# A ViT-tower kernel on one core: mixing rows on GpSimd, weight preparation spread over five prologue tiles, ballast matmuls in tile 0, energy sums ahead of the first projections

## The chip, the core and the metric

The kernel runs on one core of a Trainium2 chip, as one launch. The metric is the device time in microseconds of that core. The engines are TensorE (PE in the profile, its weight loads PEld), VectorE (DVE), ScalarE (ACT), GpSimd (POOL) and the DMA queues, of which SyncE's (SP) and ScalarE's are used. The engines run apart from each other and meet at semaphores only. Each executes its instructions in the order in which they were issued.

## What is computed

The input x has the shape (8, 512, 64, 2): 8 batches of 512 tokens with two feature sets of 64 channels, called ecg and pcg. Three stages follow each other.

```python
# stage 1: four attentions with head size D = 8 over 512 tokens
ecg_out = attn(ecg@w4, pcg@w5, pcg@w6) + alpha * attn(ecg@w1, ecg@w2, ecg@w3)
pcg_out = attn(pcg@w10, ecg@w11, ecg@w12) + gamma * attn(pcg@w7, pcg@w8, pcg@w9)
h = concatenate([ecg_out, pcg_out])                      # (8, 512, 128)
# stage 2: a reservoir and a state-space branch, on x_norm = ln(layernorm(h)), H = 256
new = tanh(xin[t] + prev @ W_res.T); prev = 0.95 * new + 0.05 * prev      # 512 steps in order
A_bar = exp(A * softplus(x_norm @ w_delta + b_delta)); B_bar = (x_norm @ W_B.T) * (1 - A_bar) / (A + 1e-8)
s = A_bar * s + B_bar
readout(s) = gelu(ln(s) @ W_ro.T + b_ro)
h = h + readout(reservoir) * gate + readout(ssm) * (1 - gate)   # gate = sigmoid(layernorm(h) @ W_gate.T + b_gate)
# stage 3: h = h + ffn(layernorm(h)); on 128 channels its additions to the output fall outside,
# and what the kernel adds for it is the normalized h
```

Alpha and gamma are inputs, b_delta too. The whole stage 2 hangs on 512 steps of the reservoir, each of which needs the one before.

## The kernel before, in words

The tokens are cut into 32 tiles of 128 tokens (8 batches times 4 quarters, the quarter outermost, so the first 8 tiles are one of each batch). For each tile the four attentions are computed on all 512 keys. The 512 steps of the reservoir then run in 32 bodies of 16 steps. Step by step TensorE, ScalarE and VectorE pass the state round, and the attention of a tile nine bodies ahead (AHEAD = 9) is laid between the steps. So nine tiles have to be made, all or in part, before the first step: that is the prologue, lines 985 to 1050 for VectorE and 1371 to 1452 for TensorE.

**The opening.** Five transfers bring the weights of the projections (wall), x by batches, the weights of stage 2 (mats) and a row of small inputs (rows, with alpha, gamma, b_delta and the reservoir's A). TensorE begins with 7 matmuls on zeros (`keep_clock`, line 1197, called ballast here: what they write is read by nothing). Then it sums the squares of the wall over the partitions. `project(b, k)` makes for batch b the queries (k = 0), keys (1) and values (2, 3) in one of two banks that alternate; it waits until VectorE has taken what lay in that bank (`stacked`). `sum_energy` adds the squares of x that ScalarE made in `square`. From this energy and the wall's norms come the scales of a batch: VectorE (`squared_scales`), GpSimd (`root`, a power of -1/2) and VectorE again (`scales`). Only then may ScalarE evacuate the batch's projections (`evacuate` waits for `scaled`). This goes for batch 0 alone first, group 1, and then for batches 1 to 7 together, group 2.

**A prologue tile j** (line 1009 for VectorE, 1395 for TensorE, 562 for ScalarE, 415 for GpSimd). `queries(j)` on VectorE subtracts the row shift from the queries, `turn_scores(j)` makes the turned scores with 16 matmuls (line 1221), ScalarE exponentiates each of the four heads twice, once to 32 bits (`prob`, line 516) and once to 16 (`prob_hi`, line 521), GpSimd subtracts them (`low_part`, line 389), and TensorE weighs the values with both parts (`weigh_high`, `weigh_low`). `sums_inverse` and `coefficients` scale the result by the mix of the two attentions: `mix_s[b]` is the row (alpha, 1, gamma, 1) over the scale of batch b, made in `mixes` by VectorE before the loop. Between these, VectorE finds the row maxima of the next tile (`top_of(j + 1, a)`, line 803), normalizes the tile before (`hat`, `hat_copy`, `normed`, `difference`), takes its gate (`gate_in`), and stacks the projections of batches j + 1 and j + 2. TensorE makes those projections in the same tile, with 6 ballast matmuls of 256 columns from tile 1 on.

**The preparation of the weights of stage 2** is on VectorE too. `row_bounds`, `all_bounds` and `take_bounds` find a bound of the weights. In tile 0, behind the third row maximum, come `prepare_weights` (lines 727 to 739: 1 over A, b_t, the readout weights times their gains, the first states of the scan) and `weight_scales` (lines 763 to 779: fifteen instructions on one column each, most of which wait for the one before through `seq`). In tile 1, behind `gate_in`, comes `weight_parts` (line 781: the identity of the carry, W_res in a high and a low half, W_in). `sum_readout` on TensorE and `readout_weights` on VectorE make the readout weights in tile 7. ScalarE and TensorE wait for `wt_ready` to reach 2 before the first step, that is, for the last of weight_parts and of readout_weights.

## Time and profile before

| | |
|---|---|
| median of 3 runs | 684.28 us (681.66 to 684.32) |
| profiled execution | 684.84 us, span 683.1 us |
| mean granted clock of TensorE | 0.959 of full |
| busy: TensorE, VectorE, ScalarE, GpSimd | 627.2, 569.6, 423.9, 192.4 us |
| chain that ended last: TensorE, VectorE, GpSimd, issue, ScalarE | 64, 12, 10, 7, 5 % |
| first fill of the scan (TensorE, line 1303) | 126.07 us |

The page gives the busy time of each engine, the chain of waits that ended last and the costliest groups. The trace behind it is read as a timeline, each line an instruction or a run of the same ones (its start, its busy time, how many, and in brackets how long the engine sat idle before it and what ended the wait), or as windows, stretches with the busy time of each engine and the granted clock of TensorE (1.00 is 2.4 GHz, 0.50 is 1.2 GHz). Neighbouring instructions of an engine overlap by the length of their latency, so the distance of two starts is what an instruction takes from its engine.

### The profile page before, as it was taken

The page shows a single profiled execution, that of the slowest core. Times are in us where ns is not written, and L with a number is a line of the kernel's source. Part 1 is how long each engine was busy: PE and PEld are TensorE (multiplying, and loading weights), DVE is VectorE, ACT ScalarE, POOL GpSimd, SP SyncE. Part 2 cuts the span into 40 slices and gives each one's busy share as a digit, 9 for nine tenths or more (in the row PEclk, how much of TensorE's full clock was granted, in tenths as well). Part 3 has the DMA queues.
Part 4 walks back from the last instruction along what each step waited for, and adds up shares of the span by engine and source line. Part 5 has one row for each costly group of instructions (what it writes and reads, how often), then busy time and mean ns, then how long its engine had stood idle before and what let it go on. Part 6 is the DMA issues. An engine that isn't in the chain of part 4 may idle for free.

```text
span 683.1 us, 28149 instructions
## 1 busy us (share of the span) xinstructions
PE 627.2 (92%) x11038; PEld 489.8 (72%) x11038; DVE 569.6 (83%) x2438; ACT 423.9 (62%) x2051; POOL 192.4 (28%) x429
## 2 busy tenths in 40 slices
PE   7778887999999999999999999999999999999762
PEld 2344554688888888888888888888887777777541
DVE  5778988688888889988998998997667888888895
ACT  4547986577766777766777776676564444444332
POOL 1233655000000000000010000001000778877776
PEclk9659998899999999999999999999999999999997
DMA  5000000000000000000000000000000000000000
GB/s 196 1 0 1 3 1 1 2 3 3 4 3 3 3 3 3 4 3 4 3 4 3 3 4 3 3 3 3 2 2 2 10 14 14 15 17 14 14 21 23
DMA packets 6324, 7.24 MB, mean 11 GB/s; under 512 B 688, under 2 KB 4784, under 8 KB 6192
## 3 DMA queue, kind: packets, MB, share of 16 engines
q1 hardware_dynamic: 5904, 4.46, 2.1%
q8 instruction: 87, 1.43, 0.9%
q10 hardware_dynamic: 288, 0.99, 0.4%
q14 instruction: 45, 0.37, 0.2%
HBM read 3.35 MB, written 2.10 MB: 8 GB/s over the span
## 4 chain that ended last, share of the span: by engine, by line
PE 64%; DVE 12%; POOL 10%; issue 7%; ACT 5%; DMA 1%; POOLq 0%; DVEq 0%; SPq 0%
PE PS L1285 23%; PE PS L1339 13%; PE PS L1297 4%; PE PS L1303 2%; PE PS L1209 2%; PE PS L1234 2%; POOL r_dev L459 2%; PE PS L1235 2%; PE PS L1241 2%; PE PS L1175 2%; PE PS L1179 2%; POOL ln_small L447 2%; PE PS L1292 2%; DVE k L1129 1%; PE PS L1198 1%
## 5 line engine op out<-in xcount | busy, mean ns | idle before, releaser
L548 ACT ACTIVATE y<-PS 128x16 f16<-128x16 f32 x512 | 93.8, 183 | 170.0 <-PE PS L1297 167.1
L1339 PE MATMUL PS<-ballast,ident 128*128 128x220 f16 (+5 forms) x722 | 151.4, 285 | 0.0
L921 DVE TENSOR_TENSOR y_lo<-ys,y 128x16 f16<-128x16 f32 x512 | 95.4, 186 | 52.6 <-ACT ys L549 48.5
L1285 PE MATMUL PS<-y_lo,res_hi 128*128 128x8 f16 x2048 | 128.7, 169 | 9.2 <-DVE y_lo L921 7.3
L1285 PEld LDWEIGHTS PS<-y,res_hi 128*128 128x128 f16 x2048 | 96.9, 97 | 55.6 <-ACT y L548 21.4
L1285 PE MATMUL PS<-y,res_hi 128*128 128x8 f16 x2048 | 129.0, 169 | 0.4 <-ACT y L548 0.3
L1285 PE MATMUL PS<-y,res_lo 128*128 128x8 f16 x2048 | 123.5, 166 | 0.0
L924 DVE SCALAR_TENSOR_TENSOR kp_lo<-PS,setup,kp 128x16 f16<-128x16 f32 x512 | 114.8, 224 | 0.0
L394 POOL TENSOR_TENSOR small<-small,minus_half 128x2 f32<-128x2 f32 x32 | 22.5, 702 | 321.5 <-DVE y_lo L921 284.9
L516 ACT ACTIVATE prob<-PS,exp_up,sc 128x512 f32<-128x512 f32 x128 | 100.3, 790 | 2.1 <-PE PS L1221 2.1
L521 ACT ACTIVATE prob_hi<-PS,exp_up,sc 128x512 f16<-128x512 f32 x128 | 100.5, 792 | 0.0
L549 ACT ACTIVATE ys<-PS 128x16 f32<-128x16 f32 x512 | 99.2, 194 | 0.0
L1285 PEld LDWEIGHTS PS<-y_lo,res_hi 128*128 128x128 f16 x2048 | 85.5, 96 | 18.8 <-DVE y_lo L921 13.8
L551 ACT ACTIVATE kp<-PS 128x16 f16<-128x16 f32 x512 | 98.3, 192 | 0.0
L803 DVE TENSOR_REDUCE top<-PS 128x1 f32<-128x512 f32 x128 | 87.0, 681 | 9.0 <-PE PS L1209 8.9
L1297 PE MATMUL PS<-kp_lo,carry_id 128*128 128x16 f16 x512 | 92.2, 180 | 0.0
L1285 PEld LDWEIGHTS PS<-y,res_lo 128*128 128x128 f16 x2048 | 87.6, 96 | 0.0
L1292 PE MATMUL PS<-kp,carry_id 128*128 128x16 f16 x512 | 86.6, 169 | 0.0
L835 DVE TENSOR_TENSOR prob_lo<-prob,prob_hi 128x512 f16<-128x512 f32 x96 | 65.3, 681 | 0.3 <-issue 0.3
L1198 PE MATMUL PS<-ballast,ident 128*128 128x512 f16 (+1 forms) x152 | 49.9, 389 | 12.6 <-DVE ys L972 9.8
L1339 PEld LDWEIGHTS PS<-ballast,ident 128*128 128x128 f16 x722 | 56.5, 97 | 0.2
L1234 PE MATMUL PS<-keep,prob_hi 128*128 128x66 f16 x512 | 50.3, 197 | 0.0
(205 smaller groups left out, 1329.3 us busy)
## 6 DMA issues: line engine op xcount, KB each, us to landing
ys<-in_x SPq DMA_DIRECT2D x8, 256.0 KB, 8.1
out<-gate_all SPq DMA_DIRECT2D x32, 64.0 KB, 1.5
mats<-in_mats ACTq DMA_DIRECT2D x1, 709.0 KB, 5.1
rows<-in_rows ACTq DMA_DIRECT2D x1, 257.5 KB, 7.9
wall<-in_wall SPq DMA_DIRECT2D x1, 256.0 KB, 4.9
```

The lines of the kernel that those rows point to most:

```text
L516: a_.activation(prob[:, a, :], X[a], ACT.Exp, scale=e_col[:, j % B:j % B + 1], bias=exp_up[:, :])
L521: a_.activation(prob_hi[:, a, :], X[a], ACT.Exp, scale=e_col[:, j % B:j % B + 1], bias=exp_up[:, :]).then_inc(prob_ready, 1)
L548: a_.activation(y16[:, :].rearrange("p (m b) -> p m b", m=NH), pre, ACT.Tanh, scale=back).then_inc(y16_ready, 1)
L549: a_.activation(ys[:, :, bass.ds(i * STEPS + (1 + t), 1)].rearrange("p (m b) o -> p m (b o)", m=NH), pre, ACT.Tanh, scale=back).then_inc(a ...
L551: a_.activation(kp16[:, :].rearrange("p (m b) -> p m b", m=NH), pre, ACT.Copy, scale=keep_scale).then_inc(kp_ready, 1)
L803: v.reduce_max(top[:, a:a + 1], X[a], AX_X).then_inc(top_ready, 1)
L921: v.tensor_tensor(y_lo[:, :], ys[:, :, bass.ds(i * STEPS + (1 + t), 1)].rearrange("p n o -> p (n o)"), y16[:, :], ALU.subtract).then_inc(l ...
L924: v.scalar_tensor_tensor(kp_lo[:, :].rearrange("p (m b) -> p m b", m=NH), PRE[t % 2][:, r, :, t // 2, :], setup[:, 24:25], kp16[:, :].rear ...
L1285: t_.matmul(dst[:, m, :], wts[:, k, m * P:m * P + P], st[:, k * B:k * B + B], start=False, stop=False, skip_group_check=True)
L1292: t_.matmul(dst, carry_id[:, :], kp16[:, :].rearrange("p (m b) -> p m b", m=NH), start=False, stop=False, skip_group_check=True)
L1297: t_.matmul(dst, carry_id[:, :], kp_lo[:, :].rearrange("p (m b) -> p m b", m=NH), start=False, stop=True, skip_group_check=True).then_inc( ...
L1339: t_.matmul(at[:, 0:size], ident16[:, :], ballast[:, 0:size], start=False, stop=True, skip_group_check=True)
```

## The change

Four edits, all of them ahead of the scan.

- **Mixing rows on GpSimd.** `mixes` leaves VectorE. GpSimd fills mix with two fills and two copies between its two roots, after the rows have landed, and signals `mix_made`; after the second root it waits for it and for the scales of group 2 and makes the eight rows mix_s, ahead of the first low part.
- **Weight preparation in pieces.** `prepare_weights`, `weight_scales` and `weight_parts` are cut into ten pieces. Tile j takes one behind `hat(j - 1)` and one behind `gate_in(j - 1)`: tile 2 reach_of_sum and powers_of_two, tile 3 inverse_powers and carry_scales, tile 4 readout_gains and weights_high, tile 5 first_states and weights_low, tile 6 input_rows and weights_in. `readout_weights` moves from the head of tile 7 to behind `difference(7)`. The product for the gate's last column moves into row_bounds.
- **Ballast in tile 0.** TensorE issues 4 matmuls of 256 columns before project(1, 0) and 8 behind project(1, 1).
- **Energies in front.** `sum_energy(0, 1, 0)` goes before `project(0, 0)`.

The ballast and the energy sums of TensorE:

```diff
@@
             t_.matmul(X[0], ones[:, :], wall_sq, start=True, stop=True).then_inc(walls_summed, 1)
+            sum_energy(0, 1, 0)
             project(0, 0)
-            sum_energy(0, 1, 0)
             project(0, 1)
@@
                 if j == 0:
+                    for n in range(4):
+                        keep_clock(MISC, 256)
                     project(1, 0)
                     project(1, 1)
+                    for n in range(8):
+                        keep_clock(MISC, 256)
```

GpSimd:

```diff
+            def mixes():
+                pool.wait_ge(mix_made, 1)
+                pool.wait_ge(scaled, 2)
+                for b in range(B):
+                    last = g.tensor_scalar(mix_s[:, b, :], mix[:, :], inv_s[:, b:b + 1], None, ALU.mult)
+                last.then_inc(mix_ready, 1)
+
             root(0, 1, 1)
+            pool.wait_ge(rows_loaded, 16)
+            g.memset(mix[:, 1:2], 1.0)
+            g.memset(mix[:, 3:4], 1.0)
+            g.tensor_copy(mix[:, 0:1], alpha_col)
+            g.tensor_copy(mix[:, 2:3], gamma_col).then_inc(mix_made, 1)
             root(1, B, 2)
+            mixes()
             for j in range(AHEAD - 1):
```

VectorE, the functions (the instructions are those of before, cut at other places; one sequenced wait moves in the scale pieces):

```diff
             def row_bounds():
+                v.tensor_tensor(gate_t[:, P:P + 1], cols[:, 0:1], cols[:, 2:3], ALU.mult)
...
-            def prepare_weights():
+            def input_rows():
                 dve.wait_ge(rows_loaded, 16)
                 seq(v.tensor_scalar(inv_a[:, :], a_row, 1e-8, None, ALU.add))
                 seq(v.reciprocal(inv_a[:, :], inv_a[:, :]))
                 v.scalar_tensor_tensor(b_t[:, :], b_raw, -1.0, inv_a[:, :], ALU.mult, ALU.mult)
+
+            def readout_gains():
                 for m in range(NH):
                     last = v.tensor_scalar(ro_s[:, m, :], ro_raw[:, m, :], ro_g_cols[:, m:m + 1], None, ALU.mult)
                 last.then_inc(ro_scaled, 1)
-                v.tensor_tensor(gate_t[:, P:P + 1], cols[:, 0:1], cols[:, 2:3], ALU.mult)
+
+            def first_states():
                 v.memset(y16[:, :], 0.0).then_inc(y16_ready, 1)
...
-            def weight_scales():
+            def reach_of_sum():
                 dve.wait_ge(bounds_taken, 1)
                 seq(v.tensor_tensor(setup[:, 22:23], setup[:, 20:21], setup[:, 21:22], ALU.mult))
                 seq(v.scalar_tensor_tensor(setup[:, 22:23], setup[:, 22:23], P / H, setup[:, 19:20], ALU.mult, ALU.add))
                 seq(v.tensor_scalar(setup[:, 22:23], setup[:, 22:23], 2.0 ** -100, None, ALU.max))
+
+            def powers_of_two():
...
+            def inverse_powers():
                 v.reciprocal(setup[:, 5:6], setup[:, 4:5])
                 seq(v.reciprocal(setup[:, 23:24], setup[:, 22:23]))
                 v.tensor_scalar(setup[:, 6:7], setup[:, 5:6], WEIGHT_UP * LEAK, None, ALU.mult)
...
+            def carry_scales():
...
+            def weights_high():
                 v.tensor_scalar(carry_id[:, :], ident[:, :], setup[:, 25:26], None, ALU.mult)
...
+                v.tensor_scalar(res_hi_flat, res_raw, setup[:, 6:7], None, ALU.mult).then_inc(hi_made, 1)
+
+            def weights_low():
                 dve.wait_ge(hi_made, 1)
...
+                v.scalar_tensor_tensor(res_lo_flat, res_raw, setup[:, 6:7], res_hi_flat, ALU.mult, ALU.subtract)
+
+            def weights_in():
+                v.tensor_scalar(in_t[:, :], in_raw, setup[:, 8:9], None, ALU.mult).then_inc(wt_ready, 1)
```

VectorE, the loop of the prologue:

```diff
             stack(0, 3)
-            mixes()
             stack(1, 0)
             for j in range(AHEAD - 1):
                 if j + 1 < B:
                     stack(j + 1, 1)
                 if j > 0:
                     hat(j - 1)
-                if j == AHEAD - 2:
-                    readout_weights()
+                if j == 2:
+                    reach_of_sum()
+                if j == 3:
+                    inverse_powers()
+                if j == 4:
+                    readout_gains()
+                if j == 5:
+                    first_states()
+                if j == 6:
+                    input_rows()
                 top_of(j + 1, 0)
...
                 top_of(j + 1, 2)
                 if j > 0:
                     gate_in(j - 1)
-                else:
-                    prepare_weights()
-                    weight_scales()
-                if j == 1:
-                    weight_parts()
+                if j == 2:
+                    powers_of_two()
+                if j == 3:
+                    carry_scales()
+                if j == 4:
+                    weights_high()
+                if j == 5:
+                    weights_low()
+                if j == 6:
+                    weights_in()
                 if j + 1 < B:
                     stack(j + 1, 3)
...
             difference(AHEAD - 2)
+            readout_weights()
             gate_in(AHEAD - 2)
```

## Rows read from the trace of the kernel before

**Rows 1.** The page: chain of waits that ended last, by engine

```profile
PE 64%; DVE 12%; POOL 10%; issue 7%; ACT 5%; DMA 1%; POOLq 0%; DVEq 0%; SPq 0%
```

**Rows 2.** Windows: stretch, busy time of each engine, then TensorE's granted clock

```profile
20.00:25.00 5.00, 3.33 (x21) 1.13 (x21) 4.56 (x24) 3.40 (x6) 1.53 (x3) 0.75 0.00 2
...
60.00:65.00 5.00, 4.42 (x44) 2.71 (x43) 4.65 (x11) 5.00 (x9) 4.51 (x5) 1.00 0.00 0
```

**Rows 3.** Timeline of the opening: start, busy, engine, line, operation, count, [idle before]

```profile
8.63 2.08 PE L1175 MATMUL PS<-ys,wall 128*128 128x512 f32 x2
...
12.45 1.03 PE L1198 MATMUL PS<-ballast,ident 128*128 128x512 f16 x4
...
8.61 0.63 ACT L493 ACTIVATE h_all<-ys 128x512 f32<-128x512 f32 x1 [5.69 <-DMA ys<-in_x]
...
13.96 0.77 ACT L502 ACTIVATE ys<-PS,k_bias,sign_s 128x512 f16<-128x512 f32 x1
...
13.12 0.16 DVE L696 SCALAR_TENSOR_TENSOR sc<-sc 128x1 f32<-128x1 f32 x1
```

**Rows 4.** Timeline of tile 0, TensorE and VectorE

```profile
20.90 0.40 PE L1221 MATMUL PS<-q_tile,k 32*128 32x128 f16 x16 [0.32 <-DVE q_tile L830]
...
40.77 2.08 PE L1175 MATMUL PS<-ys,wall 128*128 128x512 f32 x2 [3.46 <-DVE keep L707]
...
43.67 0.61 PE L1221 MATMUL PS<-q_tile,k 32*128 32x128 f16 x16 [0.50 <-DVE q_tile L830]
...
23.62 2.94 DVE L754 TENSOR_SCALAR mix_s<-mix,sc 128x4 f32<-128x4 f32 x8
```

**Rows 5.** Timeline of weight preparation in tiles 0 and 1

```profile
34.54 0.28 DVE L729 TENSOR_SCALAR inv_a<-rows 128x256 f32<-128x256 f32 x1
...
36.99 0.48 DVE L733 TENSOR_SCALAR ro_s<-mats 128x128 f32<-128x128 f32 x2
...
37.52 0.15 DVE L765 TENSOR_TENSOR setup<-setup 128x1 f32<-128x1 f32 x1
...
39.96 0.75 DVE L707 SCALAR_TENSOR_TENSOR keep<-PS,sc,keep 128x512 f16<-128x512 f32 x1
...
53.62 0.67 DVE L782 TENSOR_SCALAR carry_id<-ident,setup 128x128 f16<-128x128 f32 x1
...
54.87 0.74 DVE L787 SCALAR_TENSOR_TENSOR res_lo<-mats,setup,res_hi 128x512 f16<-128x512 f32 x1
...
56.32 1.12 PE L1175 MATMUL PS<-ys,wall 128*128 128x512 f32 x2 [1.07 <-DVE keep L707]
```

**Rows 6.** Timeline of tile 2, TensorE and VectorE

```profile
58.17 0.40 PE L1221 MATMUL PS<-q_tile,k 32*128 32x128 f16 x16 [0.31 <-DVE q_tile L830]
...
68.13 0.40 PE L1221 MATMUL PS<-q_tile,k 32*128 32x128 f16 x16 [0.29 <-DVE q_tile L830]
...
61.30 1.36 DVE L803 TENSOR_REDUCE top<-PS 128x1 f32<-128x512 f32 x2 [0.15 <-PE PS L1209]
...
66.15 0.69 DVE L803 TENSOR_REDUCE top<-PS 128x1 f32<-128x512 f32 x1 [0.26 <-PE PS L1209]
```

**Rows 7.** GpSimd in tile 2; lines 754 and 921: ns min/median/max

```profile
60.87 0.41 POOL L401 TENSOR_SCALAR small<-small 128x1 f32<-128x1 f32 x1
...
61.24 3.43 POOL L389 TENSOR_TENSOR prob_lo<-prob,prob_hi 128x512 f16<-128x512 f32 x3
...
L754 DVE TENSOR_SCALAR mix_s<-mix,sc x8: 215/218/1124, 23.6 to 26.3; 128x4 f32<-128x4 f32 x8
...
L921 DVE TENSOR_TENSOR y_lo<-ys,y x31: 135/170/493, 560.2 to 599.0; 128x16 f16<-128x16 f32 x31
```

**Rows 8.** Timeline of the readout weights in tile 7, VectorE

```profile
110.05 0.20 DVE L794 COPY ro_pair<-ident 128x128 f32<-128x128 f32 x1
...
110.37 1.13 DVE L794 COPY ro_pair<-ident 128x128 f32<-128x128 f32 x1
...
111.82 0.67 DVE L803 TENSOR_REDUCE top<-PS 128x1 f32<-128x512 f32 x1
```

More of the change, by code:

```diff
@@ L207, in build @@
         mix_ready = sem("mix_ready")
+        mix_made = sem("mix_made")
         ro_scaled = sem("ro_scaled")
@@ L743, in place_keep @@
                 v.tensor_copy(KEPT, keep_row[:, :]).then_inc(keep_placed, 1)
-            def mixes():
-                dve.wait_ge(rows_loaded, 16)
-                v.tensor_copy(mix[:, 0:1], alpha_col)
-                v.tensor_copy(mix[:, 2:3], gamma_col)
-                v.memset(mix[:, 1:2], 1.0)
-                seq(v.memset(mix[:, 3:4], 1.0))
-                dve.wait_ge(scaled, 2)
-                dve.wait_ge(const_ready, 3)
-                for b in range(B):
-                    last = v.tensor_scalar(mix_s[:, b, :], mix[:, :], inv_s[:, b:b + 1], None, ALU.mult)
-                last.then_inc(mix_ready, 1)
             def take_bounds():
@@ L774, in weight_scales @@
                 v.tensor_scalar(setup[:, 7:8], setup[:, 4:5], 1.0 / WEIGHT_UP, None, ALU.mult)
[L775 to L777 removed]
+                seq(v.tensor_scalar(setup[:, 8:9], setup[:, 5:6], WEIGHT_UP, None, ALU.mult))
+            def carry_scales():
+                v.tensor_scalar(setup[:, 25:26], setup[:, 22:23], WEIGHT_UP / CARRY_UP, None, ALU.mult)
                 seq(v.tensor_scalar(setup[:, 24:25], setup[:, 23:24], CARRY_UP * KEEP, None, ALU.mult))
+                v.tensor_scalar(setup[:, 25:26], setup[:, 25:26], setup[:, 5:6], None, ALU.mult)
                 seq(v.tensor_scalar(setup[:, 24:25], setup[:, 24:25], setup[:, 7:8], None, ALU.mult))
[L781 removed]
+            res_hi_flat, res_lo_flat = (one[:, :, :].rearrange("p k m -> p (k m)") for one in (res_hi, res_lo))
+            def weights_high():
                 v.tensor_scalar(carry_id[:, :], ident[:, :], setup[:, 25:26], None, ALU.mult)
[L783 to L785 removed]
+                v.tensor_scalar(res_hi_flat, res_raw, setup[:, 6:7], None, ALU.mult).then_inc(hi_made, 1)
+            def weights_low():
                 dve.wait_ge(hi_made, 1)
[L787 removed]
+                v.scalar_tensor_tensor(res_lo_flat, res_raw, setup[:, 6:7], res_hi_flat, ALU.mult, ALU.subtract)
+            def weights_in():
+                v.tensor_scalar(in_t[:, :], in_raw, setup[:, 8:9], None, ALU.mult).then_inc(wt_ready, 1)
             def readout_weights():
```

8 lines of the change are left out of this document (removed).

## The prediction

> **What bounds the kernel now.** I read first the page's chain of waits, which is TensorE for most of the span [rows 1]; most of that is the 512 scan steps, and the change edits nothing in them. So I read the stretch before the scan, which ends near 126 us, as tiles. A tile runs from one group of 16 turned score matmuls (line 1221) to the next. On the timeline of TensorE tile 0 runs from 20.90 to 43.67 (22.8 us), tile 1 from 43.67 to 58.17 (14.5 us) and tile 2 from 58.17 to 68.13 (9.96 us) [rows 4, 6]. Tiles 3 to 5 repeat tile 2. Tiles 0 and 1 are therefore 12.8 and 4.5 us longer than the pattern. The reasons are two. First, VectorE does work outside the pattern: mixing rows from 23.62, 2.94 us; a block of preparation from 34.54 to 39.96, 5.4 us, which leaves TensorE idle for 3.46 us before 40.77; and weight parts from 53.62 to 55.5, 1.9 us, which leave it idle for 1.07 [rows 4, 5]. Second, TensorE is at half clock: the granted clock averages 0.75 between 20 and 25 us, after a stretch in which it was mostly waiting, and the same 16 matmuls take 0.61 us at 43.67 and 0.40 at 58.17 [rows 2, 4, 6]. That is the level of 1.2 GHz against 2.4. A pair of projection matmuls shows it too: 2.08 us at 8.63 and at 40.77, 1.12 at 56.32 [rows 3, 4, 5].
>
> A tile of the pattern is nearly full on every engine: in 60 to 65 us TensorE is busy 4.42, VectorE 4.65, ScalarE 5.00 and GpSimd 4.51 us of 5 [rows 2]. VectorE's own idle time there is 0.15 us before 61.30 and 0.26 before 66.15, and some 0.2 us more while it waits for the last weighing [rows 6]. So extra VectorE work in such a tile is hidden for about 0.6 us and exposed beyond.
>
> **Opening (energies ahead of the projections).** The energy matmul leaves after the first square of ScalarE, which starts at 8.61 and with its read of the accumulator ends near 9.35; the projection now starts at 8.63 [rows 3]. The energy is then ready near 9.75, about 1.3 us sooner than now (VectorE's scale chain, which ends with line 696 at 13.12, moves with it to about 12.0). The projections start about 0.9 us later, end near 13.4 and hold the second evacuation, now at 13.96, to 13.5. Gain 0.4 us. Bounds: at best the 1.3 us of the scale chain; at worst the 0.9 us of delay plus the cold ballast of the third rival, +1.3.
>
> **Tile 0.** The mixing leaves VectorE. On GpSimd it is eight instructions of the kind of line 401 (0.41 us) [rows 7]: about 3.3 us after the scales near 22.3, so done near 25.6. What queues behind it there is the first low part, now at 23.55, which the first low weighing needs only near 29; the mixed rows themselves are needed near 33. Hidden; with that cover gone it would be 3.3. The four small fills of the mix wait for the rows transfer, before the second root: that root waits for energies at 18.6, long after, so nothing. VectorE also loses 5.4 us of preparation. With both gone and TensorE at full clock I follow the order of issue at the durations of tile 2: ballast 0.4, projections 0.95 each, ballast 0.85, then scores, weighings and projections back to back; the next turned scores come about 13.0 us after the first. Gain 22.8 - 13.0 = 9.8. The 12 added ballast matmuls cost 1.3 us of issue at full clock, 2.6 at half; VectorE and ScalarE are behind them at that point, so I count 0.3 of it, within the 13.0. The waits before 20.90 and the one for the second projection stay, so the clock may still fall near 22.5 for a few us, at a price of about 2.0 (slow projections and ballast). I take half of it, +1.0. Bounds for the tile: -12.8 (the pattern's own length) and -5.0 (only VectorE's share comes back, the clock stays low).
>
> **Tile 1.** No weight parts, full clock: the pattern, 14.5 - 9.96 = 4.5 us gained. Bound on the other side: 1.1 (only the idle piece of TensorE comes back).
>
> **The pieces, in tiles 2 to 6.** They are the same instructions. Durations by starts of the rows [rows 5]: input rows 34.54 to 36.99, 2.45; readout gains 36.99 to 37.4, 0.4; fifteen scalar columns 37.52 to 39.96, 2.4; carry and high parts from 53.62, with in_t 0.26 before line 787, about 1.25 in all; low part 0.66. By tile: tile 2 1.13, tile 3 1.27, tile 4 0.4 + 0.98 = 1.38, tile 5 0.05 + 0.66 = 0.71, tile 6 2.45 + 0.26 = 2.71; together 7.2, all of what left tiles 0 and 1.
>
> There is one price that they did not pay before. GpSimd makes the low parts of each tile from 61.24, 3.43 us for three, just behind line 401 at 60.87 [rows 7]. The first piece of a tile comes directly behind line 861, near 61.07. Where a VectorE instruction on SBUF meets such a GpSimd instruction, this trace shows it held to that instruction's end: of the eight mixing instructions of 215 ns one takes 1124; the second copy of line 794 takes 1.13 us against 0.20 for the first [rows 7, 8]; in the scan line 921 takes 135 ns at least and 493 at most once GpSimd works beside it [rows 7]. So a piece of small instructions that wait for each other can lose 1.1 us at a time.
> The Trainium skill (SBUF — State Buffer, "Who interferes with whom") says this as a rule: the port pair that VectorE and GpSimd share is an exclusive lock, held for the whole instruction, against VectorE instructions in a two-port mode or with two SBUF inputs. The trace agrees with its 1124 ns. By the rule in full each small two-input step beside the low parts waits, by a reading without it none does; the sums are the two ends below.
> I take one such wait, 1.1 us, in tiles 2 and 3 (their chained steps fall behind 61.24), none in tile 4 (its two instructions follow each other at once), none in 5 and 0.3 in 6. With the 0.6 of cover: tile 2 1.13 + 1.1 - 0.6 = 1.6; tile 3 1.27 + 1.1 - 0.6 = 1.8; tile 4 0.8; tile 5 0.1. Tile 6 issues no projections for a later tile, VectorE alone sets its end and only 0.15 is cover: 2.71 - 0.16 + 0.3 = 2.85. Sum 7.15. Bounds: without any wait 0.5 + 0.7 + 0.8 + 0.1 + 2.55 = 4.6; with six waits of 1.1, 7.2 + 6.6 - 2.6 of cover = 11.2.
>
> **Tile 7 and behind it.** The readout weights leave VectorE between 110.05 and 111.82, 1.77 us with its 0.93 us wait in line 794 [rows 8]. What is late next is TensorE's score matmul, which waits for ScalarE's exponent near 110.0: gain 1.3. Bounds 0.7 (TensorE still at half clock there, as now) and 1.8. At its new place, behind line 879 of tile 7, VectorE waits 1.3 us for the gate matmul anyway, and GpSimd has no low part left: nothing. Were that cover gone it would be 0.9. The gate column multiplied in row_bounds is 0.1 us, in the gain of the opening.
>
> **Sum.** -0.4 - 9.8 + 1.0 - 4.5 + 7.15 - 1.3 = -7.85 us. The profiled execution took 684.84 us (span 683.1 and 1.74 around it), which gives 677.0; the median of the runs shown is 684.28, 0.56 below it, and gives 676.4. I write 676.5.
>
> **Rivals.**
> 1. The pieces are cheap: no waits for GpSimd, and the clock holds through tile 0. For it: a piece delays only VectorE, and GpSimd may be the one held. Then -0.4 - 9.8 - 4.5 + 4.6 - 1.8 = -11.9: 672.4. Against it: the low parts start within 0.2 us of each piece.
> 2. The change hardly pays. The clock stays low through much of tile 0 (gain 7 there), tiles 4 and 6 wait for GpSimd too, and the idle time of TensorE that the pieces make lowers its clock for part of one tile (half of the 2.6 of rival 3): -0.4 - 7.0 - 4.5 + 9.0 - 1.0 + 1.3 = -2.6: 681.7. For it: after 20 us, where TensorE only waited for VectorE, the clock fell [rows 2]. Against it: a wait of 1.07 us in tile 1 left the clock at full.
> 3. Slower: the clock rises late at the start and falls in the prologue tiles. At the start TensorE would wait some 0.8 us for the square, between ballast and projection. The four ballast matmuls at 12.45 take 1.03 us [rows 3]; at half clock the two groups take 1.7 each and stand in front of bounds and scores: +1.3. Then the pieces drain TensorE once in each of tiles 2 to 6; a tile at half clock is 14.5 - 1.9 = 12.6 us instead of 9.96, so +2.6 in each that runs so. With tile 0 at its bound: +1.3 - 5.0 - 4.5 + 7.15 - 0.7 = -1.75 before any such tile; the first one makes the change slower, the second brings it past 0.5%: +3.45, 687.7. For it: a half-clock tile 1 is in this very trace. Against it: a pattern tile has six ballast matmuls of its own, and its TensorE is busy 4.42 of 5 us [rows 2].
>
> **Chances.** A difference under 0.5% (3.4 us) can't be told from none here: the runs shown lie 2.7 us apart. Forecast 0.50, rival 1 0.22, rival 2 0.20, rival 3 0.08. Faster takes the forecast, rival 1 and two fifths of rival 2: 0.80. Same takes most of the rest of rival 2: 0.13. Slower 0.07. The range from 670.5 to 681.8 holds the forecast with its own spread (673.5 to 680), rival 1 and about half of rival 2, some 0.85 in all.
>
> **What would show it.** Right: turned scores of tiles 0 and 1 about 13 and 10 us apart; the mixing on GpSimd with no one waiting for it; tiles 2 and 3 near 11.6, tile 4 near 10.8, tile 5 near 10.1 and tile 6 near 12.1 us; VectorE instructions of the pieces above 1 us that are 0.2 otherwise; the scan's first fill near 118.5 and a scan of unchanged length. Wrong: a granted clock of 0.5 in tiles 2 to 5, TensorE at half clock past 12.3 us in the opening, or a scan whose length moves by more than 2 us.

## The result

The changed kernel takes 673.58 us, median of 15 runs, against 682.47 of the kernel before in the same comparison. The ratio is 0.9879 with a 95% interval of [0.9856, 0.9902], so about 8.3 us are gained. The forecast was 676.5 us, from a sum of -7.85. The changed kernel's profiled execution took 672.93 us, with a span of 670.8.

The page of the changed kernel, first chain of waits by engine (answers [rows 1]), then the granted clock in 40 slices of 16.8 us; the kernel before had `9659998899` in its first ten:

```profile
PEclk9999976999999999999999999999999999999997
...
PE 61%; DVE 12%; POOL 11%; issue 9%; ACT 5%; DMA 1%; POOLq 0%; SPq 0%; DVEq 0%; ACTq 0%
```

The clock is high (9) in the first five slices and low in the sixth and seventh; before, it was low in the second and third, and less so in the seventh and eighth. The windows view, columns as in [rows 2]:

```profile
20.00:25.00 5.00, 4.25 (x36) 2.41 (x24) 3.62 (x13) 4.73 (x7) 3.10 (x9) 1.00 0.01 2
...
93.00:113.00 20.00, 17.48 (x144) 10.25 (x144) 14.22 (x48) 10.84 (x20) 7.15 (x9) 0.50 0.00 1
```

From 20 to 25 us the clock is 1.00 where it was 0.75 [rows 2]; from 93 to 113 us it is 0.50, the 1.2 GHz level.

The opening and the prologue on the timeline of TensorE (start, busy, engine, line, operation, count, [idle before]; answers [rows 3, 4, 6]; lines are those of the changed kernel):

```profile
8.97 0.38 PE L1215 MATMUL PS<-energy,ones 128*128 128x1 f32 x2 [0.97 <-ACT h_all L507]
9.21 1.96 PE L1205 MATMUL PS<-ys,wall 128*128 128x512 f32 x4
...
19.82 0.40 PE L1251 MATMUL PS<-q_tile,k 32*128 32x128 f16 x16 [0.32 <-DVE q_tile L847]
...
31.86 0.40 PE L1251 MATMUL PS<-q_tile,k 32*128 32x128 f16 x16 [0.50 <-DVE q_tile L847]
...
41.83 0.40 PE L1251 MATMUL PS<-q_tile,k 32*128 32x128 f16 x16 [0.28 <-DVE q_tile L847]
...
52.14 0.40 PE L1251 MATMUL PS<-q_tile,k 32*128 32x128 f16 x16 [0.31 <-DVE q_tile L847]
...
63.50 0.40 PE L1251 MATMUL PS<-q_tile,k 32*128 32x128 f16 x16 [0.31 <-DVE q_tile L847]
...
74.85 0.40 PE L1251 MATMUL PS<-q_tile,k 32*128 32x128 f16 x16 [0.31 <-DVE q_tile L847]
...
85.14 0.40 PE L1251 MATMUL PS<-q_tile,k 32*128 32x128 f16 x16 [0.31 <-DVE q_tile L847]
...
92.73 0.77 PE L1287 MATMUL PS<-mats,x_hat_t 128*128 128x129 f32 x2 [1.57 <-DVE xn L889]
...
97.24 0.29 PE L1244 MATMUL PS<-ident,shift_rows 128*128 128x128 f16 x1 [1.78 <-DVE shift_rows L830]
97.89 0.61 PE L1251 MATMUL PS<-q_tile,k 32*128 32x128 f16 x16
...
108.61 0.61 PE L1251 MATMUL PS<-q_tile,k 32*128 32x128 f16 x16
...
115.74 0.69 PE L1333 MATMUL PS<-xd,in_t 128*128 128x128 f32 x4
```

The differences of the starts of line 1251 are the tiles; the last row is the scan's first fill. Between 31.86 and 85.14 the 16 matmuls take 0.40 us each time, and 0.61 at 97.89 and 108.61: the clock fell at 92.7 us, with tile 6's first long wait (1.57 us) and before its second (1.78 us). The two profiles term by term, in us:

| stretch | before | after | difference | forecast |
|---|---|---|---|---|
| opening, to the first turned scores | 20.90 | 19.82 | -1.08 | -0.4 |
| tile 0 | 22.77 | 12.04 | -10.73 | -8.8 |
| tile 1 | 14.50 | 9.97 | -4.53 | -4.5 |
| tile 2 | 9.96 | 10.31 | +0.35 | +1.6 |
| tile 3 | 9.96 | 11.36 | +1.40 | +1.8 |
| tile 4 | 9.96 | 11.35 | +1.39 | +0.8 |
| tile 5 | 9.96 | 10.29 | +0.33 | +0.1 |
| tile 6 | 9.41 | 12.75 | +3.34 | +2.85 |
| tile 7 | 10.10 | 10.72 | +0.62 | -1.3 |
| from there to the first fill | 8.55 | 7.13 | -1.42 | in tile 7 |
| scan | 557.03 | 555.06 | -1.97 | 0 |

The column of differences adds up to -12.3, the difference of the spans. That is more than the 8.3 of the timed runs, because where the clock falls differs from run to run of one and the same kernel. The profiled execution of before took longer than its kernel's median (684.84 against 682.47), that of after less than its own (672.93 against 673.58).

The clock of each timed run says how large that part is. Over all runs of this study (73 of the kernel before, 6 to 14 of each other), fitted within each kernel, a mean granted clock lower by 0.010 goes with 3.8 us more. Below, "at equal clock" is a kernel's time moved by this slope to a clock of 0.975. It is a fit made after the runs; no experiment tests it. All ratios leave out one run of 1099 us, whose cause is not known, and nine of the other 199, which lie over 1.5% above the fastest of their kernel; the fit has those nine in, and without them its slope is 3.5 us, o_mix comes to 677.3 at equal clock instead of 677.7, and no other kernel moves by more than 0.3. Before: median clock 0.964 and 678.1 us at equal clock. After: 0.978 and 674.9, each with a standard error of at most 0.24. So by the fit some 3.2 us of the gain are waits that went, and 0.014 of clock, 5.3 us by the slope, is time at half clock that went.

### The profile page after: what moved, and what is told of

The parts are those of the page before. It is cut to its first block, busy times and chain, and to the rows that moved or that the text cites. A ratio compares the mean times of both kernels' runs of the same rounds, so it can differ in the third digit from the quotient of the medians.

```text
span 670.8 us, 28176 instructions
## 1 busy us (share of the span) xinstructions
PE 616.8 (92%) x11050; PEld 486.2 (72%) x11050; DVE 567.5 (85%) x2426; ACT 423.5 (63%) x2051; POOL 195.4 (29%) x441
## 4 chain that ended last, share of the span: by engine, by line
PE 61%; DVE 12%; POOL 11%; issue 9%; ACT 5%; DMA 1%; POOLq 0%; SPq 0%; DVEq 0%; ACTq 0%
PE PS L1315 24%; PE PS L1369 14%; PE PS L1327 4%; PE PS L1333 3%; POOL r_dev L473 2%; PE PS L1264 2%; PE PS L1265 2%; PE PS L1271 2%; POOL ln_small L461 2%; PE PS L1322 2%; PE PS L1239 2%; DVE k L1159 1%; DVE ys L989 1%; PE PS L1205 1%; DMA ys<-in_x 1%
## 5 line engine op out<-in xcount | busy, mean ns | idle before, releaser
L395 POOL TENSOR_TENSOR small<-small,minus_half 128x2 f32<-128x2 f32 x32 | 22.5, 703 | 317.6 <-DVE y_lo L938 282.5
```

## Experiments

Each kernel but one is the changed kernel with one edit. Tiles are read as in the table above; "fill" is the scan's first fill. Ratios are to the kernel before.

| kernel | ratio and interval | tile 0, 1 | tiles 2 to 6 | tile 7, then to fill | equal clock |
|---|---|---|---|---|---|
| the change | 0.9879 [0.9856, 0.9902] | 12.04, 9.97 | 10.31 11.36 11.35 10.29 12.75 | 10.72, 7.13 | 674.9 |
| u_mix | 0.9958 [0.9922, 0.9994] | 17.17, 9.96 | 11.39 11.35 11.35 10.28 12.74 | 10.72, 7.13 | 678.6 |
| u_mix_b24 | 0.9926 [0.9893, 0.9959] | 14.07, 9.96 | 11.40 11.35 11.35 10.29 12.75 | 9.03, 6.39 | 678.0 |
| mix_later | 0.9936 [0.9905, 0.9967] | 13.61, 13.37 | 11.39 11.35 11.35 10.27 12.76 | 9.12, 6.39 | 677.8 |
| o_mix | 0.9937 [0.9902, 0.9972] | 18.56, 14.50 | 9.99 9.96 9.96 9.96 9.42 | 10.33, 8.45 | 677.7 |
| u_ballast | 0.9887 [0.9855, 0.9920] | 12.03, 9.97 | 10.30 11.36 11.35 10.28 12.75 | 9.12, 6.38 | 675.4 |
| u_energy | 0.9915 [0.9888, 0.9942] | 12.83, 9.98 | 10.30 11.36 11.36 10.28 12.75 | 9.02, 6.38 | 676.2 |
| u_prep | 0.9907 [0.9876, 0.9939] | 17.63, 12.91 | 9.99 9.97 9.96 9.96 9.41 | 8.77, 6.38 | 676.1 |
| gains_b | 0.9864 [0.9821, 0.9906] | 12.04, 9.97 | 11.77 10.82 11.74 10.34 12.22 | 10.72, 7.48 | 676.7 |
| head_late | 0.9891 [0.9857, 0.9926] | 12.04, 9.97 | 12.34 11.01 12.40 10.44 9.66 | 11.20, 6.42 | 675.0 |
| late_rows | 0.9844 [0.9800, 0.9888] | 12.04, 9.97 | 10.29 11.36 11.34 10.29 9.67 | 11.21, 6.34 | 674.0 |
| b_late_b7 | 0.9868 [0.9826, 0.9911] | 12.04, 9.96 | 11.77 10.81 11.74 10.34 9.93 | 10.95, 7.58 | 676.2 |
| u_readout | 0.9913 [0.9888, 0.9937] | 12.03, 9.97 | 10.30 11.35 11.35 10.29 12.74 | 10.60, 6.31 | 675.3 |

### The mixing

**u_mix** puts the mixing back on VectorE. The first line below is in GpSimd's program, the others in VectorE's; the function and its four small fills move along.

```diff
             root(1, B, 2)
-            mixes()
...
             stack(0, 3)
+            mixes()
             stack(1, 0)
```

> The changed kernel with the mixing of rows back on VectorE, between the stacks of tile 0. My account: the eight instructions meet GpSimd's low parts again and take 2 to 3 us in front of the stack of batch 1, so tile 0 grows from 12.0 us to 14 to 15 and the time by about 2.5 us; tile 1 on unchanged if the clock holds. Rival: VectorE has 0.6 us waits on ScalarE in this place and the mixing hides behind ScalarE's exponents: tile 0 within 0.5 us of 12.0, time unchanged.

It gives back two thirds of the gain: 681.1 against 682.26 for the kernel before, and 3.7 us more than the change at equal clock. Tile 0 is longer than the 14 to 15 us expected. On its timeline, columns as above, VectorE:

```profile
22.52 3.04 DVE L759 TENSOR_SCALAR mix_s<-mix,sc 128x4 f32<-128x4 f32 x8
```

and TensorE behind it:

```profile
26.27 1.25 PE L1209 MATMUL PS<-wall,ys 128*128 128x256 f32 x4 [1.87 <-DVE keep L705]
```

The windows view of the same kernel:

```profile
27.50:34.00 6.50, 6.50 (x38) 3.56 (x38) 3.39 (x5) 3.38 (x5) 2.14 (x2) 0.50 0.01 3
```

TensorE waits 1.87 us for VectorE, and then comes a stretch in which it is busy all of 6.50 us at a clock of 0.50. Tile 0 is 17.17 us instead of 12.04. The kernel before has the same wait, 1.69 us at 27.26. Most of the mixing's time is itself waiting: of its eight instructions in the kernel before two take 1.11 and 1.12 us beside GpSimd's low parts and the other six 0.22. In the changed kernel the same work is 2.20 us, and nobody waits; the timeline of its GpSimd:

```profile
21.90 2.20 POOL L418 TENSOR_SCALAR mix_s<-mix,sc 128x4 f32<-128x4 f32 x8 [2.80 <-DVE sc L710]
24.06 2.27 POOL L390 TENSOR_TENSOR prob_lo<-prob,prob_hi 128x512 f16<-128x512 f32 x2
```

**u_mix_b24** asks how much of the 5.1 us is the wait and how much the clock: as u_mix, with 24 ballast matmuls behind the second projection instead of 8.

```diff
                     project(1, 1)
-                    for n in range(8):
+                    for n in range(24):
                         keep_clock(MISC, 256)
```

> The mixing on VectorE at its old place, as in the first experiment, with 24 ballast matmuls instead of 8 behind project(1, 1), to fill the 1.9 us in which TensorE then waited for VectorE. If part of the 5.1 us was TensorE's half clock from 27.4 us on, the clock now holds and tile 0 comes to about 15 us (12.0 and the 3.0 of the mixing). If the mixing's wait alone made it, tile 0 stays at 17.2.

Its timeline of TensorE, and then its window:

```profile
23.70 2.78 PE L1228 MATMUL PS<-ballast,ident 128*128 128x256 f16 x24
26.50 1.13 PE L1209 MATMUL PS<-wall,ys 128*128 128x256 f32 x4
```

```profile
27.50:34.00 6.50, 6.21 (x62) 3.47 (x61) 4.74 (x11) 4.54 (x7) 2.31 (x2) 1.00 0.00 0
```

The ballast fills the wait, the same 6.50 us are at clock 1.00, and tile 0 is 14.07. So of 17.17 - 12.04 = 5.13 us, 2.03 are the wait for VectorE and 3.10 the clock that fell behind it. The median comes down from 681.1 to 676.69, though the intervals of the two ratios overlap.

All three kernels with the mixing on VectorE also have a tile 2 of 11.39 or 11.40 us instead of 10.31, where no edit is. One instruction of the first piece makes it, a step on one column (line 771 in u_mix, 772 in the changed kernel). The timelines of VectorE and GpSimd in u_mix, then VectorE in the changed kernel, whose GpSimd row starts at 44.93:

```profile
50.02 1.16 DVE L771 SCALAR_TENSOR_TENSOR setup<-setup 128x1 f32<-128x1 f32 x1
```

```profile
50.00 1.16 POOL L390 TENSOR_TENSOR prob_lo<-prob,prob_hi 128x512 f16<-128x512 f32 x1
```

```profile
44.90 0.16 DVE L772 SCALAR_TENSOR_TENSOR setup<-setup 128x1 f32<-128x1 f32 x1
```

In the changed kernel it starts 0.03 us ahead of the low part and takes 0.16 us, in u_mix 0.02 behind it and takes 1.16. So 1.08 us of what u_mix costs is such a meeting in tile 2, and not the mixing's own time.

**mix_later** keeps the mixing on VectorE but issues it later in tile 0, where the mixed rows are just about to be needed.

```diff
                 if j > 0:
                     gate_in(j - 1)
+                else:
+                    mixes()
```

> The changed kernel with the mixing back on VectorE, but behind the third row maximum of tile 0 instead of in front of the stack of batch 1. If the place is what cost 5.1 us (TensorE's projections of batch 1 hang on that stack), tile 0 is 12.0 to 13.3 us here although VectorE makes the rows. If the engine is what counts (VectorE's 1.0 us of instructions and 1.9 us of waiting for GpSimd's low parts anywhere), tile 0 is 14.5 us or more.

Its timeline of TensorE at the end of tile 0, and a window of tile 1:

```profile
31.86 1.13 PE L1206 MATMUL PS<-ys,wall 128*128 128x512 f32 x2 [1.38 <-DVE keep L708]
```

```profile
34.00:43.50 9.50, 9.46 (x60) 5.75 (x52) 6.13 (x18) 6.93 (x12) 4.90 (x6) 0.50 0.00 1
```

Tile 0 is 13.61 us, but the wait of 1.38 at its end is followed by half clock in tile 1, which takes 13.37. 13.61 lies between the two ranges that were to decide between place and engine. Both count: neither place on VectorE is free, and the later one saves in tile 0 and pays in tile 1. On GpSimd there is no such wait.

**o_mix** does the mixing edit alone, on the kernel before (the diff is u_mix reversed).

> The kernel before with one edit of the change alone, the mixing on GpSimd. Taking the mixing back out of the changed kernel cost 5.1 us in tile 0. Theory 1 (VectorE's order in front of batch 1's stack is what counts, and TensorE's clock multiplies it): here too tile 0 loses 3 us of waiting, from 22.8 to 18 to 19.5, and since the block of preparation stays the clock still falls at some point: time 3 to 5 us under the kernel before. Theory 2 (the mixing only pays once the block of preparation is gone): tile 0 within 1 us of 22.8, time unchanged.

678.35 against 681.53, most of it by the clock (0.970 against 0.964; 0.4 us at equal clock, or 1.0 by the slope of 3.5). In its profile tile 0 is 18.56 instead of 22.77. Its span is not compared, since TensorE ran at clock 0.50 from 481.5 to 501.9 us, in the scan. TensorE's longest wait in tile 0, for the preparation block, stays, on its timeline:

```profile
35.60 2.08 PE L1176 MATMUL PS<-ys,wall 128*128 128x512 f32 x2 [4.56 <-DVE keep L721]
```

The mixing is worth about 0.6% alone and 0.8% when taken out of the whole. Taken out of the whole it is the largest part: the others cost 0.1 to 0.4%, with intervals that overlap the change's. No other edit was run alone on the kernel before.

### Ballast in the first tile

**u_ballast** takes out the 12 added matmuls.

```diff
-                    for n in range(4):
-                        keep_clock(MISC, 256)
                     project(1, 0)
                     project(1, 1)
-                    for n in range(8):
-                        keep_clock(MISC, 256)
```

> The changed kernel without the 12 ballast matmuls of tile 0. My account: TensorE's clock falls in tile 0 as before the change, its projections take 2.1 us again, tile 0 is 14 to 16 us and the time 2 to 4 us longer. Rival: without the block of preparation TensorE is busy enough, the clock holds, and tile 0 is 11.5 us, 0.5 shorter, since the eight matmuls behind project(1, 1) stand 0.6 us in front of project(1, 2).

Tile 0 takes 12.03 us without them and 12.04 with them, at full clock both times; the two intervals overlap almost wholly. Both sides of the expectation were wrong: tile 0 neither grew to 14 nor shrank to 11.5. In this kernel the 12 matmuls neither cost nor bring anything that these six runs can show. Once the mixing is gone, the longest wait in tile 0 is 0.75 us, so there is no long one for them to fill.

### The energies

**u_energy** puts the projection in front of the energy again.

```diff
-            sum_energy(0, 1, 0)
             project(0, 0)
+            sum_energy(0, 1, 0)
```

> The changed kernel with the first energy sum back behind project(0, 0). My account: the first turned scores start 0.4 us later than 19.8 (up to 1.1), all else the same, time +0.4 to +1.1. Rival: the 1.1 us by which they started earlier came from TensorE's clock having risen earlier in that profile, and the edit itself gives nothing: start unchanged at the same clock.

The ratio is 0.0036 above the change's, at equal clock the time is 1.3 us above (standard errors 0.35 and 0.24), and the intervals overlap. Its first turned scores come at 21.45, but its clock was at half from 15.0 us on, as the window shows:

```profile
15.50:25.00 9.50, 9.06 (x40) 5.60 (x40) 5.46 (x21) 3.72 (x6) 2.97 (x7) 0.50 0.00 1
```

Over the profiles this start lies between 19.81 and 21.51 whatever the edit. It is 19.94 in o_mix, which has the energy behind, with a clock that rose at 7.0 us, and 19.82 in the changed kernel, where it rose at 7.3: 0.1 us apart. So whether the order itself gains, or keeps the clock up more often, or neither, stays open.

### The pieces

**u_prep** puts all preparation but the readout weights back in tiles 0 and 1.

```diff
+                if j == 0:
+                    input_rows()
+                    readout_gains()
+                    first_states()
+                    reach_of_sum()
+                    powers_of_two()
+                    inverse_powers()
+                    carry_scales()
+                if j == 1:
+                    weights_high()
+                    weights_low()
+                    weights_in()
```

> The changed kernel with all ten pieces back in tiles 0 and 1 (the readout weights stay behind tile 7). My account: tiles 2 to 6 return to about 9.96, 9.96, 9.96, 9.96 and 9.4 (6.6 us less together), tile 0 grows by the 5.4 us block and, because TensorE then waits 3 us and its clock falls, by more, tile 1 by 2 to 4: net +1 to +4 us. Rival: the pieces cost as much as they give, and the gain is the ballast and the mixing alone: time within 1 us or lower.

Its timeline of TensorE in tile 0, and the window behind that row:

```profile
36.24 2.08 PE L1197 MATMUL PS<-ys,wall 128*128 128x512 f32 x2 [4.37 <-DVE keep L721]
```

```profile
36.50:43.00 6.50, 5.96 (x32) 2.93 (x32) 3.85 (x15) 4.38 (x8) 1.89 (x3) 0.50 0.01 1
```

Tiles 0 and 1 are 5.59 and 2.94 us longer, tiles 2 to 6 together 6.77 shorter: 1.8 us net. Tile 7 and its tail are 2.7 us shorter than in the changed kernel's profile, mostly by the clock (see tiles 6 and 7 below), so that from the first turned scores to the fill u_prep's profile is even 0.9 us shorter (94.98 against 95.92). At equal clock it is 1.2 us slower, and the intervals overlap: whether spreading gains anything is not shown. If it does, it is little, since nearly all of it comes back as VectorE time in tiles that VectorE already fills.

Whether GpSimd holds VectorE there was a step of the forecast. The changed kernel's timeline of VectorE has line 896 (not a piece: the pattern's own difference) in tiles 2 and 3, and line 750 in tile 4. The second fence is GpSimd's low part beside each line 896:

```profile
47.12 0.40 DVE L896 SCALAR_TENSOR_TENSOR xd<-xn 128x128 f32<-128x128 f32 x1
...
57.42 1.40 DVE L896 SCALAR_TENSOR_TENSOR xd<-xn 128x128 f32<-128x128 f32 x1
...
66.37 1.42 DVE L750 TENSOR_SCALAR ro_s<-mats 128x128 f32<-128x128 f32 x2
```

```profile
47.16 1.27 POOL L390 TENSOR_TENSOR prob_lo<-prob,prob_hi 128x512 f16<-128x512 f32 x1
...
57.42 1.16 POOL L390 TENSOR_TENSOR prob_lo<-prob,prob_hi 128x512 f16<-128x512 f32 x1
```

In tile 2 VectorE is 0.04 us ahead and takes 0.40; in tile 3 both start at 57.42 and VectorE takes 1.40. This 1.0 us is most of why tile 3 is longer by 1.40 us and tile 2 by 0.35. In tile 4 the two instructions of line 750, 0.48 in [rows 5], take 1.42, with a low part that starts at 66.55. The small steps of the pieces on one column and one input were not held: lines 783 to 785 of tile 3, from 55.27 us beside a low part that starts at 55.20, take 0.14 or 0.15 us each.

**gains_b** moves all pieces to the later place in their tile, behind gate_in.

```diff
                 if j == 2:
+                    reach_of_sum()
                     powers_of_two()
...
                 if j == 4:
+                    readout_gains()
                     weights_high()
```

> The changed kernel with all pieces of tiles 2 to 6 behind gate_in, none behind hat. Lock theory (a VectorE instruction with two SBUF inputs or a copy-like one on SBUF waits for the end of GpSimd's low part): the first pieces now run after the three low parts of a tile; line 896 of tile 3 (1.40 us) and line 750 of tile 4 (1.42 for two) go back to 0.55 and 0.48; tiles 3 and 4 shrink from 11.36 to about 10.4 each, tile 2 stays near 10.3, tile 6 near 12.0: 2 to 3 us less in all. Rival (the tiles are long because VectorE is full, no lock): tile lengths unchanged within 0.2 us, since the same instructions run.

Its timelines of VectorE and of GpSimd:

```profile
49.27 1.12 DVE L772 SCALAR_TENSOR_TENSOR setup<-setup 128x1 f32<-128x1 f32 x1
...
58.87 0.54 DVE L896 SCALAR_TENSOR_TENSOR xd<-xn 128x128 f32<-128x128 f32 x1
...
71.83 1.41 DVE L750 TENSOR_SCALAR ro_s<-mats 128x128 f32<-128x128 f32 x2
```

```profile
49.22 1.16 POOL L390 TENSOR_TENSOR prob_lo<-prob,prob_hi 128x512 f16<-128x512 f32 x1 [0.62 <-ACT prob_hi L535]
...
71.80 1.16 POOL L390 TENSOR_TENSOR prob_lo<-prob,prob_hi 128x512 f16<-128x512 f32 x1 [0.47 <-ACT prob_hi L535]
```

Line 896 is free again (0.54, as in the kernel before) and tile 3 falls to 10.82. But in tile 2 an instruction of one column (line 772) is now held to 1.12, and line 750 in tile 4 meets a later low part and is held as long as before. Tiles 2 and 4 are 1.46 and 0.39 longer, tiles 3 and 6 about 0.5 shorter each, and tiles 2 to 6 together 0.83 longer. The held one-column instruction ends with the GpSimd one that started just before it (49.27 + 1.12 = 50.39; 49.22 + 1.16 = 50.38). The waits move, and their sum does not fall. At equal clock the kernel is 1.8 us slower; its timed ratio is no worse than the change's, so that rests on the fit.

The Trainium skill (SBUF — State Buffer, "Who interferes with whom") names a VectorE instruction with two SBUF inputs as one that an exclusive port lock can hold; line 896 with 1.40 against 0.40, and line 772 with 1.12, agree.

**head_late** issues the pieces at the head of the tile, ahead of the keys' stack, where no low part runs, and input_rows in tile 7.

```diff
             for j in range(AHEAD - 1):
+                if j == 2:
+                    reach_of_sum()
+                    powers_of_two()
...
                 if j + 1 < B:
                     stack(j + 1, 1)
```

> The changed kernel with the pieces of tiles 2 to 5 at the head of the tile, behind the moments, where GpSimd has no low part in work, weights_in left in tile 6 and input_rows in tile 7. Lock theory: no instruction of a piece above 0.8 us; the tiles are then 10.3 (tile 2), about 10.5 (tile 3), 10.7 (tile 4), 10.1 (tile 5), together 1.5 us less than with the pieces behind hat; time 1 to 2 us under the kernel with input_rows moved alone. Rival: the low parts move with the pieces and lock the difference of line 896 instead, or the keys' stack in front of the first score is what the head delays: no gain over it.

Its timeline of TensorE in tile 2:

```profile
45.78 0.39 PE L1235 MATMUL PS<-k,keep 32*128 32x512 f16 x1 [1.46 <-DVE k L718]
...
47.17 1.97 PE L1205 MATMUL PS<-wall,ys 128*128 128x256 f32 x4
```

No piece of tiles 2 to 5 is held, yet tiles 2 and 4 are the longest of all, 12.34 and 12.40: the stack comes late, TensorE waits 1.46 us for it, and the clock falls behind the wait (the projection at 47.17 takes 1.97 where it takes 1.11 at full clock), and in tile 4 again. Tiles 2 to 5 take 2.9 us more than in late_rows below, which has the same late input_rows and its pieces in the changed kernel's places. Work in front of what TensorE waits for cost more here than work that is held behind it, and the rival that named the keys' stack was right.

### Tiles 6 and 7

The changed kernel's timeline of VectorE in tile 6:

```profile
88.01 0.29 DVE L744 TENSOR_SCALAR inv_a<-rows 128x256 f32<-128x256 f32 x1
88.34 1.75 DVE L745 RECIPROCAL inv_a<-inv_a 128x256 f32<-128x256 f32 x1
90.12 0.74 DVE L746 SCALAR_TENSOR_TENSOR b_t<-mats,inv_a 128x256 f32<-128x256 f32 x1
...
92.62 1.07 DVE L896 SCALAR_TENSOR_TENSOR xd<-xn 128x128 f32<-128x128 f32 x1
```

The 2.8 us are exposed in full, and the 1.57 and 1.78 us of idle TensorE in the timeline above come with them.

What the half clock behind these waits costs is not fixed. u_mix_b24, mix_later, u_ballast and u_energy have the same tile 6 (12.75 or 12.76 us) and the same first wait, but there the clock is at 0.50 for 6.8 us only (from 96.2 us in u_ballast, 2.7 us before its tile 7, where the changed kernel's fell 5.2 us before), and tile 7 with its tail takes 15.40 to 15.51 us. In the changed kernel and in u_mix it is at 0.50 for 20.5 us and they take 17.85. No edit of theirs is in these tiles, so the 2.4 us belong to the point at which the clock happened to fall, and not to an edit. The window in u_ballast:

```profile
96.50:103.00 6.50, 4.76 (x36) 3.13 (x37) 3.59 (x15) 3.98 (x9) 2.37 (x4) 0.50 0.01 3
```

**late_rows** moves input_rows to tile 7.

```diff
-                if j == 6:
+                if j == 7:
                     input_rows()
```

> The changed kernel with one piece moved, input_rows (one over A and b_t, 2.8 us of VectorE) from tile 6 to the same place of tile 7. Theory: tile 6 sits on VectorE alone and pays 2.8 us for it, while VectorE waits 1.2 to 2.2 us in tile 7: tile 6 from 12.75 to about 10.0, tile 7 longer by 1 to 2, and TensorE's clock, which fell during the 1.6 and 1.8 us waits of tile 6, holds longer: fill of the scan 1 to 3 us earlier. Rival: the 2.8 us are paid wherever they stand, since tile 7 too ends with VectorE: fill unchanged within 0.5 us at the same clock.

A window that holds its tile 6, and VectorE's timeline in tile 7:

```profile
85.00:96.00 11.00, 8.47 (x111) 5.29 (x109) 9.73 (x31) 8.59 (x16) 5.68 (x6) 1.00 0.00 0
```

```profile
98.51 1.75 DVE L745 RECIPROCAL inv_a<-inv_a 128x256 f32<-128x256 f32 x1
```

Tile 6 falls from 12.75 to 9.67 and stays at full clock; tile 7 is 11.21, and the clock still falls in it. With the stretch to the fill, 27.22 us instead of 30.60, of which the half clock in the changed kernel's tile 7 is some 2.4 (10.72 + 7.13 against 9.03 + 6.39 in u_mix_b24). It has the best ratio of all kernels here, 0.9844, and 0.9 us less at equal clock (standard errors 0.5 and 0.24). Its interval overlaps the change's, so it is likely and not shown to be better.

**b_late_b7** is gains_b with input_rows in tile 7 and 8 ballast matmuls in tile 6.

```diff
                 weigh_low(j, 3)
+                if j == 6:
+                    pe.wait_ge(gate_raw, j)
+                    for n in range(8):
+                        keep_clock(MISC, 256)
                 turn_shift(j + 1)
```

> All together: pieces of tiles 2 to 6 behind gate_in, input_rows in tile 7, and 8 ballast matmuls of 256 columns in front of the last turned shift of tile 6, where TensorE waits for VectorE. If lock and clock are what the pieces cost: tiles 2 to 6 near 10.3, 10.4, 10.4, 10.3 and 9.7, clock at full into tile 7, fill of the scan near 111 to 112 and the time 3 to 4 us under the changed kernel. If VectorE's own work sets the tiles: fill within 1 us of 114.4 to 115.7.

The clock holds to 104.2 us instead of 92.7, then falls all the same, and tiles 2 and 4 keep the price of gains_b: 0.9868, no gain over the change where 3 to 4 us were expected. It mixes gains_b with two further edits and can't say what the ballast alone brings.

**u_readout** puts the readout weights back ahead of tile 7's top.

```diff
                     hat(j - 1)
+                if j == AHEAD - 2:
+                    readout_weights()
...
-            readout_weights()
             gate_in(AHEAD - 2)
```

> The changed kernel with the readout weights back at the head of tile 7. My step says 1.3 us for moving them: tile 7 longer by 0.7 (TensorE at half clock there) to 1.3, the tail of the prologue unchanged, 0.7 to 1.3 us in all. Rival: in the changed kernel VectorE waits 1.4 us for TensorE's score at this place, because the clock is low, and the move gives nothing: tile 7 and tail within 0.3 us at the same clock.

Its timeline of VectorE in tile 7:

```profile
101.11 1.10 DVE L811 COPY ro_pair<-ident 128x128 f32<-128x128 f32 x1
...
104.36 1.36 DVE L896 SCALAR_TENSOR_TENSOR xd<-xn 128x128 f32<-128x128 f32 x1
```

The wait of [rows 8] is back (1.10), and tile 7 with its tail is 16.91 us against 15.40 to 15.51 in u_mix_b24, mix_later, u_ballast and u_energy. The clock fell twice here (94.4 to 101.2 and 104.6 to 111.5 us) and once in those, so 1.5 us is what the edit is worth with the clock that comes with it, and its own part may be less. The timed ratio, 0.9913, does not tell it from the change's.

## Why the prediction was right, and where it was not

**Opening, -0.4:** measured -1.08, of which the order alone shows 0.1 at like clock. The sum got the sign right by a term that the runs can't confirm. The feared worst case, cold ballast in front of the scores, did not come in this profile, whose clock rose at 7.3 us instead of 12.3. It did come in two others with the same opening: in b_late_b7 the clock rose only at 15.4 and the first turned scores start at 21.37, in u_prep it was at half from 8.9 to 15.7 and they start at 21.51, both later than the 20.90 of before. So the -1.08 is one draw of a start that varies by 1.7 us.

**Tile 0, -9.8 and +1.0:** the pattern-paced count was 13.0 us and the tile took 12.04. I had given 1.0 to a half clock at 22.5 us, since the wait for the second projection stays. The clock held. This term is half of the error of 1.93, and the count of 13.0 is the other half. My reason for the term was weak as well: I read TensorE as mostly waiting before the clock fell, but from 18.0 to 22.5 us it was busy 2.77 us of 4.50, and in the changed kernel only 2.37, and there the clock held. Why it held stays open. A wait one projection later, of 1.87 us, is followed by half clock in u_mix. That the mixing, and not the 5.4 us block of preparation, was the largest part stands nowhere in the sum: it was priced as 2.94 us of VectorE, and u_mix with u_mix_b24 showed 2.03 of wait and 3.10 of clock. I also read one of its eight instructions as held; two were, for 1.11 and 1.12 us.

**Mixing on GpSimd, 3.3 hidden:** hidden, and 2.20 us. The eight are 0.27 us apart, not 0.41 as line 401, which was the wrong row to take: it works on one element of each partition where these work on four, and yet it is the slower one.

**Tile 1, -4.5:** measured -4.53.

**The pieces, +7.15:** measured +6.81. The total was right, partly by luck. The lock waits are real and number two above the pattern, as forecast, but in tiles 3 and 4 and not in 2 and 3. The reason given, chained small steps behind 61.24, was wrong. In the kernel before line 879, the same instruction as 896, starts 1.97 us behind the first low part of its tile; the pieces make that 2.19 in tile 2 and 2.22 in tile 3, where the third low part starts, and 0.03 us decide whether it is held. In tile 4 the two wide instructions for which I took none were held. That tile 2 got none was luck too: in u_mix the same piece is held there for 1.16 us. Tile 6 was 0.5 over its 2.85: b_t takes 0.74, and line 896 is held for 1.07 there as well.

**Tile 7, -1.3:** the edit is worth up to 1.5 (u_readout), but the tile with its tail gained only 0.8. The step left out what the waits of tile 6 do to the clock: it was at 0.50 from 92.7 to 113.2 us. With the shorter half clock of u_ballast and three others the two stretches gained 3.1 to 3.25 us, so the forecast of 1.3 lies between two outcomes that it did not name. Rival 3 named this mechanism and priced it for each of tiles 2 to 6. In the changed kernel it came once, in the one tile that issues no projections for a later one, so that VectorE alone sets its end.

**The scan, 0:** -1.97 in the profiles, just inside the 2 us that I had called a sign of being wrong. It is 555.1 to 559.5 us over all but o_mix (563.5), and half-clock stretches in it come and go. From 310 to 330 and from 460 to 480 us the granted clock was 0.91 before and 1.00 after; in u_ballast it was at 0.50 from 335 to 345 us. No edit touches the scan.

The timed gain of 8.3 is close to the sum of 7.85, and partly by luck. Term by term the profiles gave 12.3: the opening and tile 0 2.6 more than forecast, the scan 2.0, the pieces 0.3, and tile 7 with its tail 0.5 less. The timed runs show 4 us less than that, because the profile of before, from which the sum started, had more half clock than its median run and that of after less. What was right is the path: VectorE's work ahead of TensorE in tiles 0 and 1, and most of its price paid again in tiles 2 to 6.

## What to carry to other kernels

Price a wait of the bottleneck engine with the clock that follows it: here 2.0 us of wait cost 3.1 more by half clock, and it was the mixing's 3 us on VectorE, not the larger block behind it, that carried most of the change. Ballast was worth its place in such a wait (24 matmuls, 3.10 us); where the waits were short, 12 matmuls changed nothing. Where two engines contend, a piece's price is not its own length: ask which instructions it shifts against the other engine, and move work only where the receiving tile has room.

## What the runs showed of the hardware

- The first rise of TensorE's clock lay between 5.5 (u_prep) and 15.4 us (b_late_b7) over profiles whose openings are the same or differ in the order of the energy sums and the place of one small product. It sometimes fell again within the opening (15.0 to 25.2 us in u_energy, 8.9 to 15.7 in u_prep). The first turned scores moved by up to 1.7 us with it.
- A VectorE instruction was held to the end of a GpSimd one that started up to 0.05 us ahead of it or at the same time (1.12, 1.16, 1.40 and 1.41 us), and not by one that started 0.03 or 0.04 us after it (0.16 and 0.40 us). Steps on one column with one input were not held beside such an instruction (0.14 and 0.15 us in tile 3).
- Within one kernel, 0.010 of mean granted clock went with 3.8 us of 673. That much clock is 13.5 us at 0.50 instead of 1.00; were TensorE's pace the limit throughout, they would cost 6.7 us. So, as an estimate, a little over half of what the clock loses reaches the end.
- A GpSimd instruction on 128x4 (line 418) took 0.29 us, eight of them 2.20 together, and one on 128x1 (line 402) 0.41.
